# Late stages of a four-block MetaFormer kernel: the third slot's steps, and the last ones of the second, two with each attention unit

## What is computed

```python
logits = jnp.einsum('bmd,bpd->bmp', qd * scale, kd)          # L2: 32 heads x 512 rows in blocks of 256 keys
_, idx = lax.top_k(logits, TOPK)                              # 16 largest of 256
attn = jax.nn.softmax(...)                                    # over the chosen ones
out = ... @ wo_w.T + wo_b

xh = x_channels @ aux_matrix                                  # L3 conv: Hadamard in groups of 64 channels
std = jnp.sqrt(jnp.mean(xs * xs, axis=(-1, -2, -3), keepdims=True))   # one value for each image
x_clip = jnp.clip(xs, -scale, scale); xq = round(...)         # 16 levels
mask = (jnp.abs(xq - xs) <= std * TRUST)

shared_out = silu(x @ shared_gate) * (x @ shared_up) @ shared_down    # L3 ffn
probs = softmax(x @ router); combine = top 2 of 8 experts
routed_out = sum_e combine_e * (silu(x @ W_gate[e]) * (x @ W_up[e])) @ W_down[e]
```

## Time and profile before

| | us |
|---|---|
| median of 3 runs | 897.02 (894.5 to 898.59) |
| the profiled execution | 895.26 |
| its span on the core | 893.5 |
| DVE busy / PE busy in it | 567.2 / 714.9 |
| last second half of a unit ends (DVE, unit 63) | 813.45 |
| last attention product ends (PE) | 823.6 |

### The profile page before, as it was taken

The page is one execution under the profiler, slowest core; times in us unless marked ns, Lnnn a source line. Parts: engine busy times, 40 slices in busy tenths (PEclk is TensorE's granted clock), DMA queues, the critical chain, the costliest instruction groups (busy, mean ns, idle before and its releaser), DMA issues.

```text
span 893.5 us, 13790 instructions
## 1 busy us (share of the span) xinstructions
PE 714.9 (80%) x4364; PEld 570.7 (64%) x4364; DVE 567.2 (63%) x2170; ACT 336.4 (38%) x825; POOL 262.9 (29%) x323
## 2 busy tenths in 40 slices
PE   6996869899829999988859997788675676586768
PEld 5885769798617999975328884556454453353436
DVE  8989522113332551387962033899999999989774
ACT  1000524445503122211101212688685674564321
POOL 5104434212370000020220003555555534633200
PEclk9997989999959999998989999799897899998989
DMA  9802355656620356710002400000000002002020
GB/s 342 277 1 72 115 176 137 199 144 166 207 62 1 142 206 219 275 56 0 1 0 83 165 1 0 2 1 1 0 1 1 1 1 49 0 14 48 13 48 25
DMA packets 25846, 72.64 MB, mean 81 GB/s; under 512 B 2840, under 2 KB 11032, under 8 KB 22960
## 3 DMA queue, kind: packets, MB, share of 16 engines
q1 hardware_dynamic: 23728, 67.56, 23.4%
q0 software_dynamic: 2048, 4.20, 1.5%
HBM read 61.61 MB, written 10.14 MB: 80 GB/s over the span
## 4 chain that ended last, share of the span: by engine, by line
PE 50%; DVE 33%; issue 7%; POOL 5%; ACT 4%; DMA 0%; DVEq 0%; POOLq 0%; ACTq 0%
PE PB L1046 6%; PE PB L914 6%; PE PB L928 5%; PE PB L1255 5%; DVE X L2340 4%; DVE arena L2591 3%; DVE top L2602 3%; PE PB L842 3%; DVE top L2586 3%; DVE arena L2605 3%; PE PB L832 2%; PE PB L1433 2%; POOL arena L654 2%; DVE XT L1943 1%; PE PB L791 1%
## 5 line engine op out<-in xcount | busy, mean ns | idle before, releaser
L783 POOL TENSOR_TENSOR arena<-arena 128x512 f32<-128x512 f32 x64 | 81.3, 1271 | 121.8 <-ACT arena L1888 121.8
L1342 PE MATMUL PB<-ring 128*128 128x256 f32 x256 | 75.9, 424 | 18.1 <-ACT arena L1880 17.3
L587 POOL TENSOR_TENSOR lnrs<-lnve,mhalf 128x4 f32<-128x4 f32 x20 | 20.8, 1038 | 228.8 <-DVE lnve L1926 228.4
L1567 PE MATMUL PB<-w_first,arena 128*128 128x128 f32 x256 | 45.3, 305 | 51.1 <-POOL arena L783 50.7
L1629 ACT ACTIVATE arena<-PB,arena 128x128 f32<-128x128 f32 x212 | 59.9, 367 | 60.7 <-PE PB L914 54.0
L1888 ACT ACTIVATE arena<-arena,nmx 128x256 f32<-128x256 f32 x128 | 58.2, 506 | 58.2 <-DVE arena L2605 57.8
L1567 PEld LDWEIGHTS PB<-w_first,arena 128*128 128x128 f32 x256 | 31.5, 153 | 75.8 <-POOL arena L783 71.0
L914 PE MATMUL PB<-arena 128*128 128x128 f32 x424 | 60.7, 289 | 13.8 <-issue 11.7
L1342 PEld LDWEIGHTS PB<-ring 128*128 128x128 f32 x256 | 48.0, 208 | 30.3 <-issue 18.1
L914 PEld LDWEIGHTS PB<-arena 128*128 128x128 f32 x424 | 54.7, 202 | 16.4 <-issue 13.7
L928 PE MATMUL PB<-ring,arena 128*128 x424 | 60.0, 286 | 2.1 <-ACT arena L1629 1.1
(11 more groups left out here) (327 smaller groups left out, 1589.8 us busy)
## 6 DMA issues: line engine op xcount, KB each, us to landing
ring<-in_taps_dram SPq DMA_DIRECT2D x12, 1536.0 KB
arena<-in_experts_dram SPq DMA_DIRECT2D x53, 258.0 KB
ring<-in_taps_dram SPq DMA_DIRECT2D x7, 1792.0 KB
arena<-comb_rows SPq DMA_DIRECT2D x6, 512.0 KB, 5.9
w_later<-in_later_dram SPq DMA_DIRECT2D x1, 2951.5 KB, 14.7
rows_back<-arena SPq DMA_DIRECT2D x11, 256.0 KB
ring<-in_second_dram SPq DMA_DIRECT2D x1, 2048.0 KB, 19.0
rows_there<-arena SPq DMA_DIRECT2D x2, 960.0 KB, 21.5
```

Source lines behind the costliest of these rows:

```text
L783: g.tensor_tensor(PR[c % 2], E1[c % 2], E2[c % 2], ALU.subtract).then_inc(sub_ready, 1)
L1342: last = mm(PB[c % 2][:, q * 256:q * 256 + 256], QM[c // 2 % 3][:, o + P * q:o + P * q + P], Kc[:, N * s + HW * j:N * s + HW * j + HW], st ...
L1567: last = tr(PB[3][:, kt * 256 + q * P:kt * 256 + q * P + P], PR[c % 2][:, q * 256 + kt * P:q * 256 + kt * P + P], ident)
```

## The change

Until now a part advanced by one step with each unit. `QUICK = {1: 26, 2: 10}` and `due(k, c)` make part 1 take two steps with each unit from step 27 on (unit 59) and part 2 from step 11 on (unit 59, too). Part 1 ends in unit 66 and not 73. Part 2 begins its router in unit 67 and not 76. Its first product with the experts' weights and its down products move from steps 35 and 38 to 38 and 42, its final copy from 41 to 45: unit 76 and not 89. Parts 0, 3 and 4 keep their places. The router of part 2 uses bank 5, as part 1's does, and some waits on shared banks name the user that is now the last.

The first hunk with a line number is PE's loop. POOL's, ACT's (for `follow_early` and for `follow`) and DVE's have the same edit. The hunks from 1407 to 1522 are PE's, 1853 is ACT's, 2561 DVE's.

```diff
+QUICK = {1: 26, 2: 10}
+
+def due(k, c):
+    d = c - PARTS[k][2]
+    q = QUICK.get(k, UNITS + TAIL)
+    return (d,) if d <= q else (2 * d - q - 1, 2 * d - q)
@@ -1557,7 +1568,8 @@
                 for k in reversed(range(len(PARTS))):
-                    follow(k, c - PARTS[k][2])
+                    for d in due(k, c):
+                        follow(k, d)

@@ -1407,8 +1417,10 @@
-                    elif k == 3:
-                        pe.wait_ge([lg_read, lg_read, pt_ready, po_ready][i], [UNITS, UNITS, UNITS, 2 * SLOTS][i])
+                    elif k == 3 and i == 3:
+                        pe.wait_ge(combT_ready, 2 * SLOTS + 3)
+                    elif k == 3:
+                        pe.wait_ge([lg_read, lg_read, pt_ready][i], UNITS)
...
                 elif d == 10:
-                    elif k < 3:
+                    elif k < 4:
                         pe.wait_ge(*at(xn_ready[7], k))
-                    elif k == 3:
-                        pe.wait_ge(ms_ready, 3)
                     else:
-                        pe.wait_ge(*at(xn_ready[7], 3))
+                        pe.wait_ge(ms_ready, 4)
                     part_turn(6, k, PB[4])
...
                 elif d == 24:
-                    if k < 2:
+                    if k < 3:
                         pe.wait_ge(ms_ready, k + 1)
-                    elif k < 4:
-                        pe.wait_ge(ms_ready, k + 2)
+                    elif k == 3:
+                        pe.wait_ge(ms_ready, 5)
...
                 elif d == 26:
-                    bank = PB[5 if k == 1 else 2]
-                    if k == 1:
-                        pe.wait_ge(po_ready, 7)
+                    bank = PB[5 if k in (1, 2) else 2]
+                    if k in (1, 2):
+                        pe.wait_ge(po_ready, k + 6)
...
-                    if d == 38:
+                    first = 42 if k == 2 else 38
+                    if d == first:
                         pe.wait_ge(gus_ready, 4 * k + 4)
                         pe.wait_ge(gu_ready, 5 * k + 5)
-                    if 38 <= d <= 40:
+                    if first <= d <= first + 2:
@@ -1853,8 +1865,8 @@
-                elif d == (41 if k < 3 else 36):
+                elif d == [41, 41, 45, 36, 36][k]:
                     final_copy(k, PB[6 if k < 3 else 4])
@@ -2561,14 +2575,15 @@
-                    if 35 <= d <= 38:
-                        combine(k, d - 35)
+                    first = 38 if k == 2 else 35
+                    if first <= d <= first + 3:
+                        combine(k, d - first)
```

More of the change, by code:

```diff
@@ L1500, in follow @@
                 elif d == 26:
-                    bank = PB[5 if k == 1 else 2]
-                    if k == 1:
-                        pe.wait_ge(po_ready, 7)
+                    bank = PB[5 if k in (1, 2) else 2]
+                    if k in (1, 2):
+                        pe.wait_ge(po_ready, k + 6)
                     elif k == 0:
                         pe.wait_ge(x_after_attn, 2)
-                    elif k == 2:
+                    elif k == 3:
                         pe.wait_ge(x_after_attn, 5)
@@ L1524, in follow @@
                         gates(k, (d - 26) // 2)
-                    if d == 38:
+                    first = 42 if k == 2 else 38
+                    if d == first:
                         pe.wait_ge(gus_ready, 4 * k + 4)
                         pe.wait_ge(gu_ready, 5 * k + 5)
-                    if 38 <= d <= 40:
-                        down(k, 2 * d - 76, PB[6])
-                        down(k, 2 * d - 75, PB[6])
+                    if first <= d <= first + 2:
+                        down(k, 2 * (d - first), PB[6])
+                        down(k, 2 * (d - first) + 1, PB[6])
                 else:
@@ L1855, in follow @@
                 elif d == 31:
-                    comb_copy3(k, PB[5 if k == 1 else 2])
-                elif d == (41 if k < 3 else 36):
+                    comb_copy3(k, PB[5 if k in (1, 2) else 2])
+                elif d == [41, 41, 45, 36, 36][k]:
                     final_copy(k, PB[6 if k < 3 else 4])
@@ L1883, in _ @@
                 for k in reversed(range(len(PARTS))):
-                    follow_early(k, c - PARTS[k][2])
+                    for d in due(k, c):
+                        follow_early(k, d)
                 if c < UNITS:
@@ L2563, in follow @@
                 elif d == 28:
-                    router_start(2, k, some, PB[5 if k == 1 else 2])
+                    router_start(2, k, some, PB[5 if k in (1, 2) else 2])
                 elif d == 30:
@@ L2596, in _ @@
                 for part in reversed(range(len(PARTS))):
-                    follow(part, c - PARTS[part][2])
+                    for d in due(part, c):
+                        follow(part, d)
                 if c < UNITS:
```

## The result

The changed kernel takes 926.94 us (median of 4 runs, 923.11 to 928.71), the kernel before 897.32 us beside it (4 runs, 894.5 to 898.59): a ratio of 1.036, with a 95% interval of 1.031 to 1.041. It is 30 us slower, and 927.0 was forecast. The profiled execution took 928.44 us for a span of 926.6 us. Medians and ratios in this document leave out runs more than 1.5% longer than the fastest of the same kernel: two of the six of e14_all_three (922.5 and 926.44 us) and one of the six of e15_part1_step_later (912.62 us).

A forecast was written before the change was run, and what follows sets the result against it. DVE bounds the kernel with its work unchanged, so its waits decide: 42.1 us against 16.4 (+25.7, taken as 25), plus 5 for PE's clock, gives +30 us, 927 us against the median; forecast range 922 to 931.

The forecast's parts named there:

- five signs: Profile after: 5 us logits wait, attention end 830 to 838, router gap 10, Hadamard gap 5, DVE's busy time as before.
- third slot's router: Units 65 to 67: DVE waits for a PE, ACT, PE chain with nothing beside it, 12.4 us, the largest term.
- unit 59, logits and tanh: Second slot's router in unit 59: DVE waits 5.6 us for PE's logits, then 1.2 us for ACT's tanh.
- unit 60: Attention, unit 60: the router's selection covers the tanh, leaving DVE a wait of 0.1 us.
- unit 64, POOL's addition: Unit 64: the third slot's statistics wait for POOL's last addition to X, 1.9 us.
- fourth part's gates: Tail: waits of 0.8 us, where interleaved down products no longer stretch these gates.
- 5 for the clock: PE bursts behind gaps (units 59, 64, 65, third slot's down products) run slow: 0 to 8 us, 5 taken.
- The change does nothing: Rival, whole kernel: cross-engine waits pin everything where it was, 897 us; chance 0.04.
- faster: Rival, whole kernel: interleaving pays as moved steps fill DVE's gaps, total waits below 16.4 us, 888 us; chance 0.05.
- The gap at unit 65 is short: Rival, before the third slot's router: PE reaches the logits some other way, 915 us; chance 0.13.
- More waits than I count: Rival: DVE's delay reaches ACT and PE again at each unit, two more of 3.5 and 12 in the tail, 946 us; chance 0.08.
- The clock falls everywhere: Rival: 3 us more in the named bursts and some at each turn of the gates, 934 us; chance 0.18.

The follow-up runs named there:

- e14_all_three: Changed kernel with part 1 doubled one step later, ahead of part 2 on PE, part 2's down products behind the last part's sum, and idle PE products: 908.14 us, ratio 1.011.
- e15_part1_step_later: Kernel before with only part 1 taking two steps per unit, from its step 28 on: 904.09 us, ratio 1.011.
- e8_filled_gaps: Changed kernel with idle products, never read, in PE's gaps ahead of part 2's Hadamard product, sum and turn and parts 1 and 2's down products: 917.43 us, ratio 1.027.
- e10_one_step_later: Changed kernel with part 1 doubled from step 28 (unit 60) and ahead of part 2 in PE's loop in units 60 to 66: 914.89 us, ratio 1.025.
- e9_downs_behind_sum: Changed kernel with part 2's down products moved behind part 4's sum of squares on PE: 923.59 us, ratio 1.032.
- e11_later_and_filled: Changed kernel with e10_one_step_later's edits and idle PE products ahead of part 2's turn and the down products of parts 1 and 2: 913.75 us, ratio 1.017.

## Why the prediction was right, step by step

*The mechanism.* Each of the five signs came: DVE waits 5.67 us for the logits near 790 us; the attention's last second half ends at 837.3 us (830 to 838 was said, 833.6 the value; it is late by two waits, of units 60 and 61, and by DVE's own slower products); the third slot's router waits 14.66 us, and the last attention product ends at 849.7; part 2's down products run ahead of the last part's Hadamard product, with a wait of 8.14 us; DVE's busy time is as before but for 2.7 us.

*The waits, term by term.*

| where | predicted, us | measured, us |
|---|---|---|
| unit 59, logits and tanh | 5.6 + 1.2 | 5.67 + 1.17 |
| unit 60 | 0.1 | 2.27 + 0.39 |
| unit 61 | 3.5 | 1.78 + 3.05 + 0.46 |
| units 62 and 63 | 1.2 + 0.8 | 1.45 + 0 |
| unit 64, POOL's addition | 1.9 | 0 |
| third slot's router | 12.4 | 14.66 |
| its gates, weights' load | 6.7 + 1.0 | 6.72 + 0.74 |
| last part's Hadamard step, root | 6.2 + 0.7 | 8.14 + 0.66 |
| fourth part's gates | 0.8 | 1.96 |
| sum | 42.1, and 5 for the clock | 49.1 |

The terms whose work was read off whole rows (unit 59, the third slot's gates) are right to 0.1 us. For unit 59 that is partly luck: the attention logits ahead of the router's were at the lower level in the row that I read (2.04 us) and in this profile (2.05); in the second profile they were not, and the wait was 4.11. The term of unit 60 is the one that failed: I had the router's selection cover the tanh, with PE at full speed. PE had idled 3.32 us, its Hadamard product took 2.08 us and the gate product 1.92. Slow products are also in unit 61 (gate products of 1.92 us), in the third slot's router (part 1's first down products 3.78, where 1.94 is the higher level) and in the last Hadamard step (ten passes of down products in 6.47). I had named units 59, 64, 65 and the third slot's down products for the clock. The second and the last of these were slow; the gate product of unit 59 took 1.10 us and the second half of the last attention product 1.04, at the higher level, and units 60 and 61 were slow where I had none. The size of the term was about right (5 taken, 6 to 7 by e8_filled_gaps), and two of its four places were wrong. The fourth part's gates (1.96 for 0.8) have slow products ahead of them too (1.06 us for 128x256, 0.59 at the higher level); no run takes this term apart.

The Trainium skill's page "TensorE: Matmul & The Clock Gate" (What's actually happening) adds that the moment of the change varies from run to run; the 3.70 and 6.78 us above agree. By its plain rule, all four bursts slow, the forecast would have been 930 us; in this trace not all four were.

*Unit 64.* The wait was 0 because DVE was itself slow: the two small instructions at 838.52 and 839.76 us took 1.21 and 1.19 us in place of 0.17, while POOL ran the last subtraction (838.44 to 839.70) and the addition (839.66 to 840.93), and each ended with POOL's. The term of 1.9 us is there as 2.1 of DVE's own time. So an instruction's duration does not always stay, as the text ahead of the prediction has it: a wait for POOL can stand inside it. The kernel before has one such instruction, L1937, 1.21 us at 814.63.

*The balance.* The measured late stretch grew by 34.6 us where I had 30: 2.0 us of it are waits above the sum (49.1 against 47.1), 2.4 DVE's longer busy time in the stretch (76.7 against 74.3). That the medians agree to 0.1 us is partly luck: the profiled executions differ by 33.2 us (928.44 and 895.26) and the medians by 29.6, for the profiled execution of the kernel before reached unit 59 at 790.3 us, later than 11 of the 13 other kernels' did, and the median of before was 892 to 899 us on the later chips.

*The rivals.* "The change does nothing" and "faster" fell with the first comparison. "The gap at unit 65 is short" fell (14.66 us). "More waits than I count" is true in a small way, in unit 60. "The clock falls everywhere" (934 us) did not come at each turn of the gates: those of the third slot ran at the higher level, with waits of 1.85 us where I had 1.8. The advice to interleave regimes, which the Trainium skill's page "Perfetto Trace Analysis" (Optimization Strategy) gives as something that may help, did not pay here in any of five placements of the doubled steps: the late stretch grew by 10 to 35 us.

*Left open:* what part of the 14.7 us of the router's wait is the last attention product behind part 1's down products on PE. Only the part of ACT's scaling was measured. Open too are the split of the loss between the two parts and the split of e10_one_step_later's gain between the later start and PE's order.

## What to carry to other kernels

When engines take their work in program order and two steps of a chain are moved closer than one round trip to another engine (here some 5 us from DVE by ACT and PE and back), the engine that was busy begins to wait, even if the schedule gets shorter on paper. Before moving steps forward, walk the path behind the new first step engine by engine and name what else the busy engine can do meanwhile; if the answer is nothing, the whole chain is the price. In a serial tail half of a removed wait, or all of its gain, can be lost again at the next ones (e9_downs_behind_sum), so a reordering is worth what is left at the end, not the wait that it removes.

## What the runs showed of the hardware

Useless products on PE made the kernel 6 us faster where they lay in real gaps (2.43 us of them inside a 3.3 us gap brought the next product from 2.08 to 1.16 us). In an order without such gaps no gain was seen (e11_later_and_filled, e14_all_three), and no loss that is clear of chance.

PE's level in a given stretch is not repeatable between executions: eight products took 3.70 or 6.78 us behind the same instructions and nearly the same gap (1.28 and 1.45 us). The late stretch of the changed kernel has a granted clock of 0.79 where the kernel before has 0.90, and PE is busy 86.2 us in it in place of 78.2 for the same products.

Two small DVE instructions of the form 128x2 (TENSOR_SCALAR, 0.17 us elsewhere) took 1.2 us, one beside POOL's subtraction and one beside its addition, both of 128x512 operands (1.26 and 1.27 us); each ended when POOL's did. DVE's product L2555 of 128x512 took 1.38 us at 831.58 us in the changed kernel, across the end of POOL's subtraction and its first addition (831.14 to 834.09), 1.60 at 834.38 beside its second, and 0.65 us each at 842.43 us with neither. Not every DVE instruction is slowed: a MATCH_REPLACE at 819.62 us (0.41 us) and a TENSOR_REDUCE at 819.96 us (0.16 us), under POOL's subtraction of 819.60 us, took their usual time.
